# A second score pair brought forward on PE, with the routing steps, the seam to the network and the last experts' queues put in another order

## The chip, the cores and the metric

One core of a Trainium2 chip. The metric is the device time of one execution in microseconds (us), lower is better; runs are compared by their median. The engines are called PE (TensorE, matrix products), DVE (VectorE), ACT (ScalarE), POOL (GpSimd, which also issues the indirect DMAs) and SP (SyncE, which issues the other DMAs). From no change, a measurement of this kernel can tell about 0.2%.

## The reference, cut to what matters

A transformer block over 4 sequences of 512 rows of 512 columns: cross attention with 16 heads of 32 columns against a context of 256 columns, then a network of 64 routed experts (each row goes to 6 of them) and one shared expert.

```
x = x + xattn(layernorm(x), ctx_1024)          # q, k normed per head; 496 main keys and 16 dca keys,
                                               # each group with a softmax of its own, summed; then @ Wo
h = layernorm(x)
scores = softmax(h @ gate_w.T)                 # 64 experts
topk_w, topk_idx = top_k(scores, 6)            # weights normed to sum 1
buf[e, pos] = h[token]                         # at most C = 384 rows for each expert
eo = (silu(buf @ w_gate.T) * (buf @ w_up.T)) @ w_down.T     # F = 352
x = x + scattered sum of eo * topk_w + shared_swiglu(h)     # shared: FS = 704
```

All products are in fp32, made of three products of rounded parts (hi x hi, hi x lo, lo x hi), so that most matrices are cut into a `hi` part on ACT and a `lo` part on DVE.

## The kernel before, in words

The program has five instruction streams, one for each engine, written out in one order by hand and joined by semaphores. An engine runs its own stream strictly in order: whatever stands behind a waiting instruction waits too. Every function takes an index and returns at once when the index is out of range (`tile(j)`: 0 to 15, a block of 128 rows; `head(n)`: 0 to 63, one head of one sequence).

**The loop over heads.** After a front part, 16 units follow; unit u works on heads n = 4u to 4u+3, and beside them on one tile of each later or earlier stage: projections and turned keys for tiles u+4 to u+7, the turned attention output of tile u-4, its output product (`wo_product`), residual and second norm for tile u-5, and the routing of tile u-6. On PE a head is: `opened(n)` (the turned row maxima of head n, and the first pair of score products of head n+1), `half1(n)` (weigh 0 of the head before, the turned product of key block 0, weigh 1, turned product 1, and the second pair of scores of head n+1), `third_key(n)`, `fourth_key(n)`. Between them stand the products of the other tiles. The scores exist for their row maxima alone: the two banks of a pair are read by DVE (`maxima(n, half)`, lines 660 to 662), and PE may write the second pair only when the maxima of the first are taken. The maxima go back to PE to be turned (line 1403) and enter the turned products (line 1428) as four more rows; ACT takes the exp of each (line 1121).

**DVE in the loop.** Between the maxima stand `residual`, `rest` (the lo part of q or k, line 687, which waits for the hi part of ACT), `weighted` (the head's output by its sums, lines 671 to 673), `scales(u)` (the reciprocals of the norms, which POOL and ACT wait for), and the routing of one tile in pieces: `route_max`, `route_top`, `route_mask`, `take_pos`, `route_code` (lines 797 to 806), `route_slots` (812 to 818), `route_weights` (823, 825). PE makes the ranks of the routed rows in `route_pos`, from the mask and a running count that POOL keeps up (`counted_on`). POOL also joins the two outputs of each head (`join`), adds biases (`biased`, line 473), scales q and k (`scaled`, line 444) and writes the slot table by indirect DMA.

**The seam.** After unit 15, PE makes the last output products, first that of tile 11 (`WAIT1`) in two halves with the weighing of the last head between, then turns the attention output of tiles 12 to 15 (`a_last`, line 1470), with the first turned rows of the network (`transpose_chunk`) ahead of them. ACT and DVE cut these into hi and lo parts (`at_high`, `at_rest`, line 709) among the cuts of the network's first weights (`cut_x`, `cut_gu`).

**The network.** 72 items (8 of the shared expert, 64 routed ones with two blocks of 128 rows each) run in a fixed pipeline. For each routed item POOL gathers the rows, and adds the results onto the output by two indirect DMAs (`scatter`, line 2188), each pair only when the pair before has landed, since they add.

**Third blocks.** Experts with more than 256 rows (four with these inputs) get a third block each, in a loop at the end whose length is read from memory. SP loads its weights (`load`: gate and up weights, then down weights), POOL gathers and scatters (`gather`, line 2634; the scatter at line 2670 waits until the one before has landed), and the blocks 0 to 2 are started from within the last items (`gather_first`, `after`). The loads and gathers run three blocks ahead, so that some are for blocks that are not worked on.

## Time and profile before

| | |
|---|---|
| median of 3 runs | 1766.02 us (1765.25 to 1768.4) |
| the profiled execution | 1762.85 us |
| span of its instructions | 1761.1 us |
| mean granted TensorE clock | 0.982 |
| busy: PE / DVE / ACT / POOL | 96% / 62% / 58% / 43% of the span |

The span is the time from the first to the last instruction of the profiled execution. A busy PE isn't PE at its peak: a product also counts as busy at the lower clock. The share of busy time is a mean over very different parts: in the items PE has no idle time at all, in the front, at the seam and in the last 50 us it has.

### The profile page before, as it was taken

Reading aid. Unit: us, or ns where it says so; the run is one execution under the profiler, and the core shown is the slowest. Engines: PE = TensorE matmul, PEld = TensorE weight load, DVE = VectorE, ACT = ScalarE, POOL = GpSimd, SP = SyncE. Lnnn points to the kernel's source line nnn. Section 1 sums busy time; section 2 is a strip of 40 time slices with the busy share of each in tenths; the row PEclk is TensorE's granted clock in tenths of the full one; section 3 lists DMA queues with packets and bytes.
Section 4 is the critical chain, followed back from the end, with each engine's and each line's share of the span. In section 5 each row is a group of like instructions: output and inputs, shape, how many; then the busy total and the mean of one; then the engine's idle time right before and its main releaser. Section 6 shows DMA issues by size and latency. Waiting matters only on the chain. (4 is left out here: it accounts for less than half of the span.)

```text
span 1761.1 us, 35834 instructions
## 1 busy us (share of the span) xinstructions
PE 1693.0 (96%) x11782; PEld 1539.8 (87%) x11782; DVE 1090.3 (62%) x2157; ACT 1028.3 (58%) x1871; POOL 757.9 (43%) x719
## 2 busy tenths in 40 slices
PE   4899999999999999999999999999999999999995
PEld 3588888888888888989999999999999999999984
DVE  7555656777566665443666666666666666666664
ACT  4567766666545553222566666666666666666664
POOL 7513222334223230242245555555555555455554
PEclk8899999999899999999999999999999999999997
DMA  5543433433222532312577777777777777777766
GB/s 189 160 117 91 119 105 97 121 95 98 83 84 79 177 107 87 122 38 86 181 227 232 209 214 226 218 210 223 223 216 205 228 221 213 222 232 206 215 198 212
DMA packets 149083, 289.87 MB, mean 165 GB/s; under 512 B 29199, under 2 KB 66319, under 8 KB 139649
## 3 DMA queue, kind: packets, MB, share of 16 engines
q1 hardware_dynamic: 116112, 238.21, 41.9%
q0 software_dynamic: 32880, 50.51, 13.7%
q8 instruction: 50, 0.82, 0.2%
q14 instruction: 41, 0.33, 0.1%
HBM read 243.73 MB, written 64.52 MB: 175 GB/s over the span
## 5 line engine op out<-in xcount | busy, mean ns | idle before, releaser
L2188 POOL DMA_INDIRECT out<-y,ids_s x128 | 209.9, 1640 | 280.3 <-ACT y L2323 254.8
L2448 PE MATMUL ps<-xt_hi,gu_hi 128*128 128x256 f32 (+1 forms) x1856 | 303.5, 285 | 0.6 <-issue 0.6
L2448 PE MATMUL ps<-xt_lo,gu_hi 128*128 128x256 f32 (+1 forms) x1856 | 289.8, 278 | 0.0
L2448 PE MATMUL ps<-xt_hi,gu_lo 128*128 128x256 f32 (+1 forms) x1856 | 289.2, 278 | 0.0
L2223 DVE TENSOR_TENSOR gu_lo<-raw_gu,gu_hi 128x1408 fp32r<-128x1408 f32 (+2 forms) x132 | 214.6, 1625 | 112.5 <-ACT gu_hi L2220 109.3
L1121 ACT ACTIVATE prob<-ps 128x512 f32<-128x512 f32 x256 | 152.2, 597 | 191.4 <-PE ps L1428 169.6
L2448 PEld LDWEIGHTS ps<-xt_hi,gu_hi 128*128 128x128 f32 (+1 forms) x1856 | 250.6, 181 | 9.0 <-issue 3.0
L2448 PEld LDWEIGHTS ps<-xt_lo,gu_hi 128*128 128x128 f32 (+1 forms) x1856 | 244.4, 181 | 0.0
L2448 PEld LDWEIGHTS ps<-xt_hi,gu_lo 128*128 128x128 f32 (+1 forms) x1856 | 244.2, 181 | 0.0
L2168 POOL DMA_INDIRECT xg<-h_rows,ids_g x128 | 191.6, 1497 | 115.2 <-POOL ids_g L2163 50.6
L2280 ACT ACTIVATE h_hi<-h 128x256 fp32r<-128x256 f32 (+1 forms) x240 | 100.6, 419 | 224.0 <-DVE h L2349 223.4
L1447 PE MATMUL ps<-v_main,prob 128*128 128x33 f32 x1536 | 208.9, 274 | 0.0
L1447 PEld LDWEIGHTS ps<-v_main,prob 128*128 128x128 f32 x1536 | 194.8, 194 | 0.0
L660 DVE TENSOR_REDUCE nmax<-ps 128x2 fp32r<-128x992 f32 x128 | 152.2, 1189 | 58.2 <-PE ps L1418 54.4
L2271 ACT ACTIVATE sg<-ps 128x256 f32<-128x256 f32 (+1 forms) x240 | 91.0, 379 | 156.4 <-PE ps L2448 96.4
L2220 ACT ACTIVATE gu_hi<-raw_gu 128x1408 fp32r<-128x1408 f32 (+2 forms) x132 | 180.9, 1370 | 0.0
L464 POOL DMA_INDIRECT slot_table<-rows,slot x96 | 97.5, 1016 | 135.5 <-DVEq L1078 107.0
L2466 PE MATMUL ps<-d_hi,h_lo 128*128 128x512 f32 (+2 forms) x480 | 140.5, 398 | 0.0
L2349 DVE TENSOR_TENSOR h<-sg,ps 128x256 f32<-128x256 f32 (+1 forms) x240 | 99.3, 414 | 62.9 <-ACT sg L2271 55.4
L2466 PE MATMUL ps<-d_lo,h_hi 128*128 128x512 f32 (+1 forms) x480 | 137.3, 394 | 0.0
L2466 PE MATMUL ps<-d_hi,h_hi 128*128 128x512 f32 (+1 forms) x464 | 134.9, 397 | 0.0
L2354 DVE TENSOR_TENSOR h_lo<-h,h_hi 128x256 fp32r<-128x256 f32 (+1 forms) x240 | 101.2, 422 | 49.4 <-ACT h_hi L2280 48.0
(316 smaller groups left out, 3000.3 us busy)
## 6 DMA issues: line engine op xcount, KB each, us to landing
raw_gu<-in_w_gu SPq DMA_DIRECT2D x71, 1408.0 KB, 6.7
raw_d<-in_w_d SPq DMA_DIRECT2D x71, 512.0 KB
raw_d<-in_w_d SPq DMA_DIRECT2D x71, 192.0 KB
qs<-qk_rows SPq DMA_DIRECT2D x192, 64.0 KB, 2.2
ks<-qk_rows SPq DMA_DIRECT2D x192, 64.0 KB, 2.0
xa<-in_x SPq DMA_DIRECT2D x16, 256.0 KB, 3.0
qk_rows<-k_hi SPq DMA_DIRECT2D x16, 256.0 KB, 2.2
qk_rows<-k_lo SPq DMA_DIRECT2D x16, 256.0 KB, 2.5
```

Of the source, the lines that this page charges most:

```text
L660: dve.tensor_reduce(nmax[:, n % 2, t, 0], ps[:, SCB:SCB + 2, 0:MAIN], AX, ALU.max, negate=True)
L1121: act.activation(prob[:, n % 2, c, :], ps[:, STB + c % 2, :], ACT.Exp).then_inc(prob_ready.sem, 1)
L1447: last = pe.matmul(ps[:, POB, o:o + HD + 1], prow[:, c, :], v_main[:, b % 2, c, h, :], start=False, stop=c == T - 2)
L2168: pool.indirect_dma_start(out=B.xg[:, p, k, :], out_offset=None, in_=hbuf, in_offset=bass.IndirectOffsetOnAxis(B.ids_g[:, p, k:k + 1], 0), ...
L2188: pool.indirect_dma_start(out=out, out_offset=bass.IndirectOffsetOnAxis(B.ids_s[:, p, k:k + 1], 0), in_=B.y[:, p, k, :], in_offset=None, b ...
L2220: eng.activation(hi, raw, ACT.Copy).then_inc(gu_hi.sem, 1)
L2223: eng.tensor_tensor(lo, raw, hi.bitcast(F32), ALU.subtract).then_inc(gu_lo.sem, 1)
L2280: act.activation(B.h_hi[0:m, it.half, c, 0:W], B.h[0:m, (it.half * NF + c) % 2, 0:W], ACT.Copy).then_inc(h_hi.sem, 1)
L2349: dve.tensor_tensor(B.h[0:m, b, 0:W], B.sg[0:m, b, 0:W], gu_banks(it, c)[1], ALU.mult).then_inc(h_ready.sem, 1)
L2354: dve.tensor_tensor(B.h_lo[0:m, it.half, c, 0:W], B.h[0:m, (it.half * NF + c) % 2, 0:W], B.h_hi[0:m, it.half, c, 0:W].bitcast(F32), ALU.su ...
L2448: last = pe.matmul(gu_banks(it, c)[half], gu_columns(w, it, half, d, c), x[:, x_p, d, 0:W], start=i == 0, stop=i == len(steps) - 1)
L2466: last = pe.matmul(ps[:, Y0 + k % 2, :], h[0:m, p, c, k * P:(k + 1) * P], w[0:m, p, c, :], start=begins and i == 0, stop=ends and i == len ...
```

## The change

It changes no computation, only orders, in six places:

- **PE, loop.** `half1(n, early)` puts the second pair of scores of head n+1 behind the first turned product of head n instead of behind the second. It is early in head n where there is an output product (units 5 to 15), and in heads n+2 and n+3 where there is a q and k product (units 0 to 9). `route_pos` moves behind `third_key`, and `k_turned` behind it too in units 10 and on.
- **DVE, loop.** `weighted(n)` comes before `route_top`; `route_mask` behind `scales`; `route_code` behind the next maxima and `rest`; `route_slots` and `route_weights` behind `weighted(n + 2)`. POOL scales k and q before `counted_on`.
- **Seam.** The last head's four weighings come first; `a_last(WAIT1 + 1)` stands between the halves of the first output product, and both `a_last` stand before the network's first turned rows; ACT and DVE do `at_high` and `at_rest` of these before the cuts.
- **Items, POOL.** The copy of the scatter's indices is made before the wait for the last landing. The third block 2 is gathered one place earlier, and block 3 where block 2 was.
- **Third blocks.** Gathers run four ahead; down weights are loaded two ahead, behind the gate and up weights of three ahead; the weight and index columns are copied one block earlier.
- **ACT, last item.** `act_d(FIRST)` comes before `results`.

```diff
                 join(n)
                 scatter(u - 7, 2, 4)
-                counted_on(u - 6)
                 scaled(u + 5, kb, H, k_sum, kn_ready)
                 scaled(u + 5, qb, 0, q_sum, qn_ready)
+                counted_on(u - 6)
                 biased(u + 6, P, qb, bq, q_raw, q_bias)
                 join(n + 1)
                 scatter(u - 7, 4, 6)
...
                 ctx_rest(u + 6)
                 at_rest(u - 4)
                 maxima(n + 2, 1)
+                weighted(n)
                 route_top(u - 6)
-                weighted(n)
-                route_mask(u - 6)
                 maxima(n + 3, 0)
                 scales(u)
+                route_mask(u - 6)
                 maxima(n + 3, 1)
                 take_pos(u - 6)
                 weighted(n + 1)
-                route_code(u - 6)
                 maxima(n + 4, 0)
                 rest(u + 5, k_full, k_hi, k_lo, k_high, k_low, k_out)
+                route_code(u - 6)
+                maxima(n + 4, 1)
+                weighted(n + 2)
                 route_slots(u - 6)
-                maxima(n + 4, 1)
                 route_weights(u - 6)
-                weighted(n + 2)
                 summed(u + 6, sq_q, 0, q_sq, q_sum)
             item = net.item
             weighted(HEADS - 1)
+            at_rest(WAIT1 + 1)
             residual(WAIT1)
+            at_rest(WAIT1 + 2)
             net.cut_x(dve, item, 0, False)
             net.cut_x(dve, item, 1, False)
-            at_rest(WAIT1 + 1)
-            at_rest(WAIT1 + 2)
             net.cut_gu(dve, item, 0, False)
             residual(WAIT1 + 1)
             at_rest(WAIT1 + 3)
...
             item = net.item
+            at_high(WAIT1 + 1)
+            at_high(WAIT1 + 2)
             net.cut_x(act, item, 0, True)
             net.cut_x(act, item, 1, True)
-            at_high(WAIT1 + 1)
-            at_high(WAIT1 + 2)
             net.cut_gu(act, item, 0, True)
             at_high(WAIT1 + 3)
             net.cut_gu(act, item, 1, True)
...
                 shift_turned(n)
                 scores(n + 1, 0)
-            def half1(n):
+            def half1(n, early=False):
                 weigh(n - 1, 0)
                 turn_scores(n, 0)
+                if early:
+                    scores(n + 1, 1)
                 weigh(n - 1, 1)
                 turn_scores(n, 1)
-                scores(n + 1, 1)
+                if not early:
+                    scores(n + 1, 1)
             def third_key(n):
                 weigh(n - 1, 2)
...
                 if u == 5:
                     pe.wait_ge(pool_split, POOL_SPLIT["wo"])
                 wo_product(u - 5)
-                half1(n)
+                half1(n, tile(u - 5))
                 x_turned(u + 6)
                 route_logits(u - 6)
                 third_key(n)
...
                 opened(n + 2)
                 q_product(u + 6)
-                half1(n + 2)
+                half1(n + 2, tile(u + 6))
+                if tile(u + 6):
+                    k_turned(u + 5)
+                third_key(n + 2)
                 route_pos(u - 6)
-                k_turned(u + 5)
-                third_key(n + 2)
+                if not tile(u + 6):
+                    k_turned(u + 5)
                 fourth_key(n + 2)
                 opened(n + 3)
                 k_product(u + 6)
-                half1(n + 3)
+                half1(n + 3, tile(u + 6))
                 third_key(n + 3)
                 q_turned(u + 5)
                 h_turned(u - 5)
                 fourth_key(n + 3)
-
-            item = net.item
-            pe.wait_ge(at_lo.sem, at_lo.value(WAIT1, 1))
-            pe.wait_ge(h2T_in.sem, h2T_in.value(WAIT1 - 1, 1))
-            wo_half(WAIT1, 0)
-            weigh(HEADS - 1, 0)
-            weigh(HEADS - 1, 1)
-            wo_half(WAIT1, 1)
-            weigh(HEADS - 1, 2)
-            weigh(HEADS - 1, 3)
             def a_last(j, free, use):
                 pe.wait_ge(head_done.sem, head_done.value(HEADS - 1, 1))
...
                 wo_half(j, 0)
                 wo_half(j, 1)
+            item = net.item
+            for t in range(T):
+                weigh(HEADS - 1, t)
+            pe.wait_ge(at_lo.sem, at_lo.value(WAIT1, 1))
+            pe.wait_ge(h2T_in.sem, h2T_in.value(WAIT1 - 1, 1))
+            wo_half(WAIT1, 0)
+            a_last(WAIT1 + 1, v_ready, TILES - 1)
+            wo_half(WAIT1, 1)
+            pe.wait_ge(nmT_in.sem, nmT_in.value(HEADS - 1, 1))
+            a_last(WAIT1 + 2, pos_taken, GROUP1 - 1)
             pe.wait_ge(nmax_ready.sem, nmax_ready.value(HEADS - 1, 2))
             net.transpose_chunk(pe, item, 0)
             net.transpose_chunk(pe, item, 1)
-            a_last(WAIT1 + 1, v_ready, TILES - 1)
-            pe.wait_ge(nmT_in.sem, nmT_in.value(HEADS - 1, 1))
-            a_last(WAIT1 + 2, pos_taken, GROUP1 - 1)
             wo_last(WAIT1 + 1, pv_taken, HEADS - 1)
             a_last(WAIT1 + 3, at_lo, WAIT1 + 1)
             wo_last(WAIT1 + 2, x1_ready, WAIT1)
...
         if not it.exists or it.shared:
             return
         p = it.half
+        pool.tensor_copy(B.ids_s[:, p, 0:nb], slots_of(it, B.ids)).then_inc(s_copied.sem, 1)
         if it.known and it.e == SH_ITEMS:
             for k in range(nb):
                 pool.wait_ge(y_out[k].sem, y_out[k].value(TOKEN_BLOCKS // 2 - 1, 16))
         else:
             pool.wait_ge(added.sem, added.value(it.expert - 1, 16 * nb))
-        pool.tensor_copy(B.ids_s[:, p, 0:nb], slots_of(it, B.ids)).then_inc(s_copied.sem, 1)
         pool.wait_ge(y_taken.sem, y_taken.value(it.rows, nb))
         pool.wait_ge(s_copied.sem, s_copied.value(it.expert, 1))
         pool.sem_inc(passed, 1)
...
             gather(pool, it + 2)
             if not (it + 2).exists:
                 thirds["gather_first"](pool, (it + 2).e - ITEMS)
+            if not (it + 1).exists:
+                thirds["gather_first"](pool, 2)
             scatter(pool, it - 1)
         def after(it):
-            thirds["gather_first"](pool, 2)
+            thirds["gather_first"](pool, 3)
+            thirds["weight_column"](pool, FIRST)
+            thirds["row_column"](pool, FIRST)
             scatter(pool, it)
             thirds["y_freed"](pool)
...
             thirds["silu"](act, FIRST)
             thirds["act_gu"](act, FIRST + 1, 1)
             thirds["act_x"](act, FIRST + 1)
+            thirds["act_d"](act, FIRST)
             results(it)
-            thirds["act_d"](act, FIRST)
         drive(act, slot, after, side)
...
         return eng.value_load(over[0:1, bass.ds(b.j, 1)], min_val=0, max_val=E - 1)
     def sync(sp):
-        def load(e, b, gu_done, d_done):
-            src = ins["w_d"][bass.ds(e, 1)].rearrange("a f n -> (a f) n")
-            sp.wait_ge(*gu_done)
+        def load_gu(b, done, turn):
+            e = expert(sp, b)
+            sp.wait_ge(done.sem, done.value(turn, 2))
             sp.dma_start(B.raw_gu[:, b.p].rearrange("p a n -> p (a n)"),
                          ins["w_gu"][bass.ds(e, 1)].rearrange("a p n -> p (a n)")).then_inc(gu_in[b.p].sem, 16)
-            sp.wait_ge(*d_done)
+
+        def load_d(b, done, turn):
+            e = expert(sp, b)
+            src = ins["w_d"][bass.ds(e, 1)].rearrange("a f n -> (a f) n")
+            sp.wait_ge(done.sem, done.value(turn, 1))
             sp.dma_start(B.raw_d[:, b.p, 0:2, :], src[0:2 * P, :].rearrange("(c p) n -> p c n", p=P)).then_inc(d_in[b.p].sem, 16)
             sp.dma_start(B.raw_d[0:FCH[2][1], b.p, 2, :], src[2 * P:F, :]).then_inc(d_in[b.p].sem, 16)
         sp.wait_ge(A["over_made"], 1)
         for k in range(2):
-            load(expert(sp, FIRST + k), FIRST + k, (S.gu_lo.sem, S.gu_lo.value(LAST_ITEM.weights - 1 + k, 2)),
-                 (S.d_lo.sem, S.d_lo.value(LAST_ITEM.weights - 1 + k, 1)))
-        load(expert(sp, FIRST + 2), FIRST + 2, (gu_lo.sem, gu_lo.value(0, 2)), (d_lo.sem, d_lo.value(0, 1)))
+            load_gu(FIRST + k, S.gu_lo, LAST_ITEM.weights - 1 + k)
+            load_d(FIRST + k, S.d_lo, LAST_ITEM.weights - 1 + k)
+        load_gu(FIRST + 2, gu_lo, 0)
         def body(b):
-            e = expert(sp, b + 3)
-            load(e, b + 3, (gu_lo.sem, gu_lo.value(b.j + 1, 2)), (d_lo.sem, d_lo.value(b.j + 1, 1)))
+            load_gu(b + 3, gu_lo, b.j + 1)
+            load_d(b + 2, d_lo, b.j)
         each(sp, body)
     def gather(pool, b):
...
             in_offset=bass.IndirectOffsetOnAxis(B.ids3[:, b.p:b.p + 1], 0),
             bounds_check=N - 1, oob_is_err=False).then_inc(rows_in[b.p].sem, 16)
+    def weight_column(pool, b):
+        e = expert(pool, b)
+        pool.tensor_copy(B.wsl3[:, b.p:b.p + 1], B.w[:, bass.ds(e * CB + 2, 1)]).then_inc(w_copied.sem, 1)
+
+    def row_column(pool, b):
+        e = expert(pool, b)
+        pool.tensor_copy(B.ids3s[:, b.p:b.p + 1], B.ids[:, bass.ds(e * CB + 2, 1)]).then_inc(s_copied.sem, 1)
+
     def gather_first(pool, k):
         if k == 0:
...
         if k < 2:
             pool.wait_ge(S.xt_ready.sem, S.xt_ready.value(LAST_ITEM.rows - 1 + k, DC))
         else:
-            pool.wait_ge(xt_ready.sem, xt_ready.value(0, 1))
+            pool.wait_ge(xt_ready.sem, xt_ready.value(k - 2, 1))
         gather(pool, FIRST + k)
     def y_freed(pool):
...
     def gpsimd(pool):
         def body(b):
-            e = expert(pool, b)
-            pool.tensor_copy(B.wsl3[:, b.p:b.p + 1], B.w[:, bass.ds(e * CB + 2, 1)]).then_inc(w_copied.sem, 1)
-            pool.tensor_copy(B.ids3s[:, b.p:b.p + 1], B.ids[:, bass.ds(e * CB + 2, 1)]).then_inc(s_copied.sem, 1)
-            pool.wait_ge(xt_ready.sem, xt_ready.value(b.j + 1, 1))
-            gather(pool, b + 3)
+            pool.wait_ge(xt_ready.sem, xt_ready.value(b.j + 2, 1))
+            gather(pool, b + 4)
+            weight_column(pool, b + 1)
             if b.q:
                 pool.wait_ge(added.sem, added.value(b.j - 1, 16))
                 pool.sem_inc(y_free.sem, 1)
...
                 out=out, out_offset=bass.IndirectOffsetOnAxis(B.ids3s[:, b.p:b.p + 1], 0),
                 in_=B.y[:, b.p, 0, :], in_offset=None, bounds_check=N - 1, oob_is_err=False,
                 compute_op=ALU.add).then_inc(added.sem, 16)
+            row_column(pool, b + 1)
         many = each(pool, body)
         for p in range(2):
-            pool.wait_ge(rows_in[p].sem, (many + (4 - p)) // 2 * 16)
+            pool.wait_ge(rows_in[p].sem, (many + (5 - p)) // 2 * 16)
         pool.wait_ge(S.added.sem, S.added.value(LAST_ITEM.expert, 16 * nb))
         pool.sem_inc(passed, 1)
         with pool.If(many > 0):
...
             act.activation(B.y[:, b.p, 0, :], ps[:, Y0 + b.p, :], ACT.Copy, scale=B.wsl3[:, b.p:b.p + 1]).then_inc(y_taken.sem, 1)
         many = each(act, body)
         for p in range(2):
-            loads = (many + (4 - p)) // 2
-            act.wait_ge(gu_in[p].sem, loads * 16)
-            act.wait_ge(d_in[p].sem, loads * 32)
+            act.wait_ge(gu_in[p].sem, (many + (4 - p)) // 2 * 16)
+            act.wait_ge(d_in[p].sem, (many + (3 - p)) // 2 * 32)
         act.sem_inc(act_passed, 1)
     def dve_gu(dve, b, half):
```

## Rows read from the trace of the kernel before

**Rows 1.** List of waits of PE, 304 to 460 us: waited for, total, times, longest us.
```profile
PE ps L1403 <- DVEq L662: 2.6, 4, 0.8
```

**Rows 2.** Timeline, end of unit 8 and start of 9: start us, us, engine, line, operation, idle.
```profile
375.37 0.18 DVE L797 TENSOR_SCALAR tmp<-rank_of 128x64 f32<-128x64 f32 x1
...
377.05 0.22 DVE L806 TENSOR_TENSOR code<-code,tmp 128x64 f32<-128x64 f32 x1 [0.24 <-issue]
...
379.78 0.69 DVE L687 TENSOR_TENSOR k_lo<-k_full,k_hi 128x512 fp32r<-128x512 f32 x1 [1.07 <-ACT k_hi L1227]
...
380.80 1.65 POOL L473 TENSOR_TENSOR kb<-kb,bqk 128x512 f32<-128x512 f32 x1 [2.20 <-ACT kb L1129]
...
381.39 1.08 DVE L818 SCALAR_TENSOR_TENSOR slot<-code,slot_f 128x8 int32<-128x8 f32 x1
...
382.39 1.18 DVE L660 TENSOR_REDUCE nmax<-ps 128x2 fp32r<-128x992 f32 x1
...
383.75 0.61 PE L1403 MATMUL ps<-ident,nmax 128*32 128x128 f32 x4 [0.59 <-DVEq L662]
...
386.38 1.18 DVE L660 TENSOR_REDUCE nmax<-ps 128x2 fp32r<-128x992 f32 x1
...
388.23 0.48 PE L1428 MATMUL ps<-qs,ks 128*128 128x512 f32 x1
```

**Rows 3.** Timeline, unit 13.
```profile
538.49 0.41 PE L1444 MATMUL ps<-v_last,prob 128*128 128x66 f32 x2 [0.22 <-DVE pv L673]
...
541.65 1.09 ACT L1121 ACTIVATE prob<-ps 128x512 f32<-128x512 f32 x2
...
548.07 0.73 PE L1418 MATMUL ps<-ks,qs 96*128 96x512 f32 x2 [0.33 <-issue]
```

**Rows 4.** Windows: us, each engine's busy us (instructions), PE clock, DMA share, GB/s.
```profile
400.00:440.00 40.00, 39.40 (x276) 35.23 (x275) 28.60 (x78) 25.56 (x44) 15.94 (x19) 1.00 0.33 94
440.00:480.00 40.00, 38.83 (x228) 34.19 (x228) 23.29 (x63) 21.29 (x38) 12.46 (x16) 0.83 0.32 90
1000.00:1200.00 200.00, 200.00 (x1467) 188.41 (x1466) 128.60 (x225) 130.11 (x240) 109.27 (x89) 1.00 0.76 218
```

**Rows 5.** Timeline of PE, unit 10.
```profile
442.37 0.66 PE L1470 MATMUL ps<-ident,kb 128*128 128x128 f32 x4 [0.85 <-POOL kb L444]
```

**Rows 6.** Timeline, the seam.
```profile
611.50 0.60 ACT L1121 ACTIVATE prob<-ps 128x512 f32<-128x512 f32 x1 [0.96 <-PE ps L1428]
...
612.73 1.63 PE L1464 MATMUL ps<-wo,aT 128*128 128x512 f32 x6 [1.27 <-ACT h2T L1252]
...
620.57 1.09 PE L1470 MATMUL ps<-ident,ao_odd 128*128 128x128 f32 x8 [0.86 <-POOL ao_odd L453]
...
623.14 3.02 PE L1464 MATMUL ps<-wo,aT 128*128 128x512 f32 x12 [1.49 <-DVE aT L709]
...
632.17 0.69 DVE L709 TENSOR_TENSOR aT<-ps,aT 128x512 fp32r<-128x512 f32 x1
```

**Rows 7.** Timeline, the last 51 us.
```profile
1710.07 1.08 POOL L2183 COPY ids_s<-ids 128x2 int32<-128x2 int32 x1 [2.92 <-DMA out<-y,ids_s]
...
1712.01 4.75 POOL L2188 DMA_INDIRECT out<-y,ids_s  x1 [0.86 <-issue]
1712.16 3.15 DVE L2728 TENSOR_TENSOR gu_lo<-raw_gu,gu_hi 128x1408 fp32r<-128x1408 f32 x2
...
1717.07 1.83 POOL L2188 DMA_INDIRECT out<-y,ids_s  x1 [0.30 <-issue]
...
1726.18 1.96 POOL L2670 DMA_INDIRECT out<-y,ids3s  x1 [4.85 <-issue]
...
1728.11 1.12 PE L2769 MATMUL ps<-ident,xg 128*128 128x128 f32 x4 [7.59 <-DMA xg<-h_rows,ids]
...
1734.65 1.57 POOL L2670 DMA_INDIRECT out<-y,ids3s  x1 [4.09 <-ACT y L2718]
...
1751.48 1.57 POOL L2670 DMA_INDIRECT out<-y,ids3s  x1 [1.07 <-issue]
```

2 lines of the change are left out of this document (1 added, 1 removed).

## The prediction

> **What bounds the kernel now.** I read the page first. PE is busy in 96% of the span (the table above), so the kernel is a queue of matmuls and a change can only pay where PE waits, where its clock is low, or at the two ends. The table of windows over the whole span then shows where that is: the items from 760 to 1700 us have no idle at all (200 us busy of 200 [rows 4]), so nothing in them is priced; the loop over heads (85 to 612 us) has small waits, the seam behind it three, and the last 50 us are poor in PE work. The list of waits of PE in the loop names one regular wait: four times, 2.6 us in all, for the second row maxima of DVE [rows 1]. The timeline around it shows the order that causes it [rows 2], and that of later units shows two smaller ones [rows 3]. The windows show one stretch in which PE ran slowly without waiting: between 440 and 480 us the granted clock is 0.83 and only 228 matmuls fit, against 276 in the 40 us before [rows 4]; it begins behind a wait of 0.85 us [rows 5]. The timeline of the seam gives its three waits [rows 6]. For the end I read the chain that ended last and then the timeline of POOL's queue: the end is a chain of scatters, not of matmuls [rows 7].
>
> **The loop, boundaries of units 6 to 9 (heads n+3 to n+4).** The change moves the second score pair up by one weighing and one turned product (about 1.1 us), `route_code` from before `maxima(n+4,0)` to behind `rest`, and `route_slots` out to behind `weighted(n+2)`. What is late here is not the scores: DVE sits idle until ACT delivers `k_hi` (line 687 at 379.78 us), then runs `route_slots` and only then the second maxima at 382.39, for which PE waits until 383.75 [rows 2]. The order on ACT ahead of `k_hi` isn't touched, so `rest` starts at the same time, and the early scores alone gain nothing at this boundary. In place of `route_slots`, `route_code` now stands between: 375.37 to 377.27 is 1.9 us as it stands, some 1.7 without a disturbance, so 380.4 becomes 382.1. It would be done 0.3 us before the old start, if nothing stopped it. But line 818 took 1.08 us and ended with POOL's bias of `kb` (380.80 plus 1.65) [rows 2]: a DVE operation that reads two tensors of SBUF stood until POOL was through. After the change the bias comes at about 381.3 (its copy on ACT follows the exp of the second turned product, and that is 0.47 us later, since the scores stand before it), still within `route_code`, whose last four operations read two tensors each. I let it hold DVE for 1.0 us: the maxima start at 383.1 instead of 382.39, and PE waits 0.7 longer. Bounds: 0.3 gained (no collision), 1.3 lost (blocked twice). Four boundaries at 0.7: +2.8.
>
> The debt is carried on. From the end of line 660 at 383.6 to its next end at 387.6 DVE needed 4.0 us; with `route_slots` (1.2 us: 380.4 to 382.5 less 0.9 of blocking) it needs 5.2. PE reaches the early second scores at the end of the turned product at 388.23, so at 388.55, which is 4.8 us after 383.75 [rows 2]. So in the next head they wait some 0.4 us, where before they stood 1.1 us later and found the maxima done. Three boundaries, those whose unit still has a `summed` for q: +1.2 (bounds 0 and +2.4). Behind PE there, everything waits. At the boundary from unit 10 to 11 there is a `rest` for k but no bias: `route_code` is 0.5 longer than `route_slots`: +0.5. Part sum **+4.5**, bounds -1.2 and +8.
>
> **The loop, units 10 to 15.** Here the second scores keep their place (the test is on `tile(u + 6)`), but DVE's new order counts. In unit 13 PE waits 0.33 us at 548.07 for maxima that ran behind `route_code`; without it they end about 1.2 us sooner and the wait goes. The model of the profile gives 0.33, the starts of neighbouring products 0.5 more than usual; I take 0.45, four times: -1.8. At 538.49 PE waits 0.22 for `weighted(n)`, which now stands ahead of `route_top`. That gain is mostly lost again: `route_pos` no longer stands between the second and third turned product, and the third needs the exp at 541.65, late because of the table loads of `deviations` [rows 3]. I take -0.15 for each of five units. Part sum **-2.55**, bounds -4 and 0. Units 0 to 4 have no routing and no such waits: 0. At the heads with `q_product` or `k_product` in front, these cover the first maxima, so that the early scores find them done; without that cover each would cost up to the 1.2 us of line 660. In head n of units 5 and on, `wo_product` is the cover, apart from the 0.4 above.
>
> **Unit 10 and the clock.** PE waits 0.85 us for the scaled `kb` [rows 5]; 2 us later the clock is at its lower level, 1.2 GHz, and stays there: a mean of 0.83 over 40 us is 13.6 us at half, and 48 matmuls fewer than before at 0.145 us each are 7 us, of which 0.85 is the wait itself [rows 4]. I take 6.1 us. After the change the product of `kb` comes one weighing and one turned product (1.6 us) later, so that it finds `kb` (there at 442.37), and `counted_on` steps out of the way of the scaling. That removes the wait; but the third turned product steps up and waits some 0.5 for its exp (in unit 13 it would stand at 541.7, and the exp at 541.65 takes 0.5), and `route_pos` may wait for a mask that DVE now makes behind `scales`. So the idle is split, not gone: 0 for the wait itself (bounds -0.85 and +0.9), and for the clock **-6.1** if it stays up and 0 if it does not. Two waits of half the length, with a full product between them, speak for staying up. So does the seam, where 1.27, 0.86 and 1.49 us of idle within 12 us did not bring the clock down [rows 6].
>
> **The seam.** The idle is 1.27 (for `h2T`), 0.86 (for POOL's last join) and 1.49 us (for `aT_lo` behind two cuts) [rows 6], 3.6 in all. The weighings of the last head now come first and wait only for its last exp (611.50 plus 0.60), some 0.7 us; half an output product then hides `weighted` and the join, and `at_rest` ahead of the residual hides the third. What is late next is `at_rest(WAIT1 + 4)`: at 632.17 plus 0.69 it was just in time, and everything before it has now moved up by 3 us while the cuts ahead of it on DVE have not become shorter: 0.4 to 0.6. The first gate product moves up by **2.6** (bounds 1.0 and 3.6), and the weight loop behind it, PE-bound, keeps that.
>
> **The end.** Four experts have a third block. Their scatters start 8.4 us apart, each once the one before has landed: the first at 1726.18, the second at 1734.65, the fourth at 1751.48; 9.6 us after it the span ends [rows 7]. PE's wait of 7.59 us for gathered rows (1728.11) looks like the prize: POOL could gather that block only behind the scatters of the last routed expert, and now gathers it one place earlier. But the second scatter, whose product stood behind that wait, came 8.5 us after the first, no later than the fourth behind the third: the wait was hidden under the landing. What counts is when the last routed expert's scatters land. Their copy of indices started at 1710.07 as the scatter before landed, took 1.08, and the issue came at 1712.01; with the copy ahead of the wait it comes at about 1710.95. It then lasted 4.75 us, against 1.57 at 1734.65, because DVE ran two subtractions from 1712.16 to 1715.31 [rows 7]. These move up too, by some 1.7 us, the length of `act_d`, which ACT now does while it would wait for the results (an estimate). I take 1710.95 + 4.3 + 0.3 + 1.6 = 1717.2 at the one end, 1715.3 (it slips in between the two) at the other, against 1718.90: 1.7 to 3.6, so **-2.5**. The further `gather` on POOL (2 to 3 us) lies under the 8.4 us. SP now issues the gate and up weights without waiting behind the down weights, so they compete with these scatters earlier and less at the very end (one load of down weights is gone, one gather more): bounds for the part 0 and -5.
>
> The Trainium skill (SBUF — State Buffer, Who interferes with whom) says that a `tensor_tensor` with two SBUF inputs takes only the read side of the port that DVE shares with GpSimd, and infers that the making of descriptors isn't stopped by it. By that sentence the issue at 1712.01 would not have been held; the row of 4.75 us speaks against it. Under it the part would be that of rival (5).
>
> **Sum.** +4.5 - 2.55 - 6.1 - 2.6 - 2.5 = -9.25, against the profiled execution (1762.85, span 1761.1) 1753.6. The median of the runs shown is 3.2 us above it; I put the difference on the median: **1756.8 us**.
>
> **The rivals.** (1) The clock falls all the same, at unit 10 or at one of the boundaries, where PE now stands 1.3 to 1.7 us: all else as forecast, 1762.9. For it: the fall behind 0.85 us. Chance 0.34. (2) The other side: the boundary wait of units 6 to 9 itself brings the clock down, unit after unit. Each fall costs 6.1 us; with two it is 1769, with three 1775, so it decides from the third on, or from the second with the boundaries at the top of their bound. Against it: 1.27 us at the seam did nothing. 0.13. (3) `route_code` isn't stopped by POOL and the scores don't wait: the boundaries give -1.2, 1751.1. Against it: line 818. 0.12. (4) PE's wait at the end was real: -7.6 in place of -2.5, 1751.7; the scatters' even spacing speaks against it. 0.03. (5) DVE doesn't hold the issue: two of 1.57 us from 1710.95 end at 1714.4, so -4.5 at the end, 1754.8; 0.04, as the 4.75 us speak against it. My forecast: 0.34 as well, but with its neighbours (3) to (5), which differ by 6 us at most, by far the larger side.
>
> **How the numbers follow.** The forecast's own range is 1753 to 1761. The range for 8 in 10 takes in (3) to (5) below and (1) with its scatter above, 1751.5 to 1766.5, and leaves out (2) and the tails. From no change a measurement can tell about 0.2%, 3.5 us: faster is below 1762.5, slower above 1769.5. Faster: forecast, (3), (4), (5) and four tenths of (1): 0.65. Slower: the greater part of (2), and a little for unseen costs: 0.13. Same: 0.22.
>
> **What would show it.** The wait for the second maxima at the unit starts should grow from 0.6 to 0.8 us to about 1.4, with DVE's line 801 to 806 stretched beside POOL's bias; if it is gone, part one is wrong. Scores in head n of units 7 to 9 should wait about 0.4 us. The 0.33 waits in heads n+3 of units 11 to 14 should be gone. The clock between 100 and 700 us should be 1.00 throughout; a single 0.5 stretch makes it rival (1). The first gate product should start some 2.6 us earlier than the sum of the loop's changes says, and the four last scatters should still be 8.4 us apart with no wait of PE for rows before them. The prediction is wrong if the clock falls again, or if loads that start earlier push the landings apart.

## The result and the profile after

The changed kernel is slower by some 1%: 1784.64 us (median of 4, 1781.12 to 1787.78) against 1765.63 us (median of 4), a ratio of 1.0114 with a 95% interval of 1.0087 to 1.0141. The forecast was 1756.8 us. The profiled execution of the changed kernel took 1782.14 us, its span is 1780.4 us and its mean granted clock 0.969, against 1762.85, 1761.1 and 0.982.

The local prices come first, since they held. The list of waits of PE in the changed kernel, 300 to 460 us and then 460 to 620 us, answers to [rows 1, 3]:

```profile
PE ps L1403 <- DVEq L662: 5.4, 4, 1.4
PE ps L1418 <- DVEq L662: 1.4, 4, 0.4
PE ps L1428 <- ACT prob L1121: 0.7, 1, 0.7
```

```profile
PE ps L1428 <- ACT prob L1121: 1.8, 4, 0.5
```

The boundary wait is 1.4 us where 1.4 was forecast. The early scores wait 0.4 where 0.4 was, though four times and not three. The third turned product waits 0.5 for its exp as expected, in unit 10 it waits 0.7. The waits of 0.33 in head n+3 are gone. The timeline at the end of unit 8 shows the cause as forecast: DVE's line 803 was held until POOL's bias was through.

```profile
382.59 1.14 DVE L803 SCALAR_TENSOR_TENSOR code<-rank_of,code 128x64 f32<-128x64 f32 x1
...
382.31 1.34 POOL L473 TENSOR_TENSOR kb<-kb,bqk 128x512 f32<-128x512 f32 x1 [2.63 <-ACT kb L1129]
```

What failed is in the windows, which answer to [rows 4] (columns as there; the clock is the third number from the end):

```profile
400.00:440.00 40.00, 38.25 (x260) 33.93 (x258) 29.11 (x65) 23.05 (x42) 15.10 (x17) 1.00 0.33 96
440.00:480.00 40.00, 39.34 (x214) 34.89 (x213) 23.35 (x59) 20.48 (x36) 11.37 (x14) 0.74 0.27 77
480.00:540.00 60.00, 58.33 (x419) 51.70 (x417) 41.53 (x114) 33.20 (x55) 17.77 (x24) 1.00 0.30 84
540.00:580.00 40.00, 39.38 (x232) 35.00 (x231) 23.42 (x62) 18.09 (x33) 10.26 (x13) 0.79 0.22 64
580.00:620.00 40.00, 39.55 (x231) 35.12 (x230) 23.79 (x64) 19.21 (x33) 11.23 (x15) 0.79 0.54 185
620.00:660.00 40.00, 37.51 (x188) 32.32 (x187) 22.00 (x55) 16.33 (x24) 12.86 (x15) 0.79 0.14 47
660.00:700.00 40.00, 39.62 (x314) 37.58 (x314) 20.34 (x44) 21.68 (x45) 5.22 (x5) 1.00 0.27 93
```

PE is as busy as ever, but makes 232 products between 540 and 580 us where 279 fit at the rate of 480 to 540 (419 in 60 us). The clock record of the trace puts PE at its lower level (1.2 GHz) from 446.9 to 467.3, 549.3 to 566.3, 586.8 to 603.9 and 627.8 to 644.8 us: 71.7 us in four stretches, where the kernel before has one of 13.7 in this part (443.8 to 457.4). Such a stretch is called a fall below. Ahead of each stands a wait of the third turned product for its exp. These are the rows of units 10, 12 (no fall), 13 and 15:

```profile
446.21 0.50 PE L1428 MATMUL ps<-qs,ks 128*128 128x512 f32 x1 [0.66 <-ACT prob L1121]
...
517.44 0.50 PE L1428 MATMUL ps<-qs,ks 128*128 128x512 f32 x1 [0.46 <-ACT prob L1121]
...
547.26 0.50 PE L1428 MATMUL ps<-qs,ks 128*128 128x512 f32 x1 [0.45 <-ACT prob L1121]
547.61 0.33 PE L1540 MATMUL ps<-mask,upper 128*128 128x64 f32 x2
...
621.87 0.50 PE L1428 MATMUL ps<-qs,ks 128*128 128x512 f32 x1 [0.44 <-ACT prob L1121]
```

In units 13 and 14 the fall begins 2 us behind the start of this product, in unit 15 only 6 us behind it. The same 0.45 stands at 487.26 and 517.44 (units 11 and 12) with no fall behind it, so one such wait doesn't bring the clock down each time. By the starts of the units, unit 12, wholly at 2.4 GHz, took 30.2 us against 31.1 before the change; unit 14, with a fall, took 37.0 against 30.5.

### The profile page after: what moved, and what is told of

The parts are those of the page before. It is cut to its first block, busy times and chain, and to the rows that moved or that the text cites. A ratio compares the mean times of both kernels' runs of the same rounds, so it can differ in the third digit from the quotient of the medians.

```text
span 1780.4 us, 35877 instructions
## 1 busy us (share of the span) xinstructions
PE 1712.1 (96%) x11782; PEld 1558.7 (88%) x11782; DVE 1097.3 (62%) x2157; ACT 1030.1 (58%) x1871; POOL 778.6 (44%) x723
## 4 chain that ended last, share of the span: by engine, by line
PE 84%; issue 4%; DVE 3%; ACT 3%; DMA 2%; POOL 2%; DVEq 1%; POOLq 1%; ACTq 0%; SPq 0%
PE ps L2455 35%; PE ps L2473 18%; PE ps L1447 8%; PE ps L1455 4%; PE ps L1428 4%; PE ps L2432 3%; PE ps L1418 3%; PE ps L1444 2%; PE ps L1470 2%; PE ps L1403 1%; DMA out<-y,ids3s 1%; DMA out<-y,ids_s 1%; PE ps L2450 1%; DVE nmax L660 1%; ACT prob L1121 1%
## 5 line engine op out<-in xcount | busy, mean ns | idle before, releaser
L2191 POOL DMA_INDIRECT out<-y,ids_s x128 | 206.0, 1609 | 300.6 <-ACT y L2330 254.1
L1447 PE MATMUL ps<-v_main,prob 128*128 128x33 f32 x1536 | 217.7, 281 | 0.0
L1447 PEld LDWEIGHTS ps<-v_main,prob 128*128 128x128 f32 x1536 | 203.8, 202 | 0.0
```

Of the source, the lines that this page charges most:

```text
L1447: last = pe.matmul(ps[:, POB, o:o + HD + 1], prow[:, c, :], v_main[:, b % 2, c, h, :], start=False, stop=c == T - 2)
L2191: pool.indirect_dma_start(out=out, out_offset=bass.IndirectOffsetOnAxis(B.ids_s[:, p, k:k + 1], 0), in_=B.y[:, p, k, :], in_offset=None, b ...
```

## The experiments

Eighteen kernels ran. Each ratio is against the kernel before, timed beside them; its median there lay between 1762.3 and 1766.0 us, so that a difference of 4 us between kernels of the table that didn't run together says little. The last column names where the profiled execution ran at 1.2 GHz between the start of unit 10 and the first gate product.

| label | us, median | ratio (95%) | at 1.2 GHz |
|---|---|---|---|
| changed kernel | 1784.64 | 1.0087 to 1.0141 | units 10, 13, 14, end of 15 |
| e1_pe_order_late | 1809.28 | 1.0198 to 1.0327 | all six |
| e2_loop_as_before | 1760.19 | 0.9955 to 1.0020 | unit 10, seam |
| e3_loop_alone | 1790.23 | 1.0078 to 1.0209 | units 10, 13, 14, end of 15 |
| e4_seam_as_before | 1782.28 | 1.0083 to 1.0158 | units 13, 15 |
| e5_mask_back_too | 1808.25 | 1.0222 to 1.0261 | all six |
| e6_dve_pool_order_alone | 1803.38 | 1.0205 to 1.0259 | all six |
| e7_pe_order_alone | 1755.06 | 0.9933 to 0.9989 | seam |
| e8_waits_removed | 1800.87 | 1.0182 to 1.0226 | all six |
| e9_wait_filled | 1770.73 | 1.0003 to 1.0045 | unit 15 |
| e10_dve_head_n2_back | 1773.02 | 1.0017 to 1.0076 | units 10, 14, seam |
| e11_pe_order_and_late_boundary | 1764.06 | 0.9980 to 1.0014 | unit 14, seam |
| e12_weighted_first | 1803.83 | 1.0199 to 1.0247 | units 11 to 15 |
| e13_last_rows_first | 1756.19 | 0.9937 to 0.9981 | seam |
| e14_boundary_back_too | 1754.32 | 0.9908 to 0.9957 | seam |
| e15_pe_order_rows_first | 1756.07 | 0.9937 to 0.9982 | seam |
| e16_swap_filled | 1762.60 | 0.9983 to 1.0016 | seam |
| e17_seam_back_too | 1757.43 | 0.9939 to 0.9979 | seam, twice |
| e18_seam_filled | 1751.90 | 0.9900 to 0.9951 | none |

**Which part does it.** `e1`: in head n+2 of units 10 to 15, PE's order of before.

```diff
+                if not tile(u + 6):
+                    route_pos(u - 6)
+                k_turned(u + 5)
+                third_key(n + 2)
                 if tile(u + 6):
-                    k_turned(u + 5)
-                third_key(n + 2)
-                route_pos(u - 6)
-                if not tile(u + 6):
-                    k_turned(u + 5)
+                    route_pos(u - 6)
```

> Changed kernel with one order on PE put back, in units 10 to 15 alone: in head n+2 route_pos and k_turned stand between the second and the third turned product again, as before the change; everything else stays changed. Theory A (the four stretches at the lower clock in units 10, 13, 14 and at the seam come from the third turned product, which the change put in that place and which there waits 0.4 to 0.5 us for its exp in a stretch of small products): that wait is covered again, the granted clock between 460 and 660 us is 1.00 (at most one stretch), and the time falls by 3 or 4 times 6 to 8 us, to 1755 to 1764. Rival B (they come from DVE's order in the loop, or from the waits of 1.4 us at the boundaries of units 6 to 9): the four stretches stay and the time is 1780 to 1787. Rival C (they come from the new order of the seam): the stretches in the loop stay, 1780 or more.

> Changed kernel with the whole loop over heads as before the change, on PE, DVE and POOL; only the seam, the items' index copies, the third blocks and ACT's last item stay changed. Theory A and rival B alike: the clock in the loop is that of before, one stretch at the lower level behind unit 10, and the time is the kernel before less the two parts that lie behind the loop, 2.6 and 2.5 us in the prediction, 1759 to 1762 where the kernel before is 1765. Rival C (the seam's order brings the clock down): a stretch at the lower level at 600 to 650 us and a time of 1766 or more.

> Kernel before with the loop's part of the change alone (PE, DVE and POOL); the seam, the items, the third blocks and the end are as before. Theory A and rival B alike: the stretches at the lower clock in units 10, 13 and 14 are there, and the time is about 4 to 5 us above the changed kernel, 1786 to 1790. Rival C: no stretches of the clock beyond those of before, 1765 to 1772.

> Changed kernel with the seam as before the change (PE, DVE and ACT); the loop, the items, the third blocks and the end stay changed. Theory A and rival B alike: the stretches at the lower clock in units 10, 13 and 14 stay; the seam's own gain of 2.6 us is lost, 1785 to 1788, unless the last of the four stretches (627.8 to 644.8 us) hangs on the seam, then 1778 to 1781. Rival C: the stretches go and the time is below 1770.

`e2` and `e3` came out as A and B said (`e3` 0.2 us above its range): the loss is in the loop alone. `e2` has a fall of 6.8 us at the seam all the same. `e4` fits neither form. In its trace the third turned product waits 0.67 us in unit 10 and 0.46 in unit 14 with no fall behind either, and the last fall begins within a wait of 2.17 us for the rows of head 63 (up to 604.27 us), a cause of its own that comes back below. Theory A in its simple form fell with `e1`, which got worse by 25 us: with `route_pos` in its old place, PE waits there for a mask that DVE now makes behind `scales`. Its list of waits, 460 to 620 us:

```profile
PE ps L1540 <- DVE mask L789: 4.1, 4, 1.0
```

So the place of PE's product alone wasn't the cause; there was a longer wait behind the one that was removed.

**Which order on which engine.** `e5` is `e1` with the mask put back:

```diff
                 route_top(u - 6)
+                route_mask(u - 6)

                 maxima(n + 3, 0)
                 scales(u)
-                route_mask(u - 6)
```

> The kernel of e1_pe_order_late (route_pos and k_turned between the second and third turned product again in units 10 to 15) with one order on DVE put back as well: route_mask stands directly behind route_top, no longer behind scales. In e1_pe_order_late route_pos waited about 1.0 us for that mask in each of units 10 to 15, and the lower clock followed in each of the six. Theory A2 (in units 10 to 15 any wait of PE of some 0.5 us or more in the second half of head n+2 can bring the clock down; the change makes such a wait whichever of the two products comes first, since it moved both the product and the mask): now neither waits, no stretch at the lower clock in units 11 to 15, at most one in unit 10 (k_turned stands in its old place), and the time is 1752 to 1763. Rival B2 (the falls come from the early second scores or from the longer waits at the boundaries of units 6 to 9, which are still there): the stretches stay, 1780 to 1800.

> The kernel of e2_loop_as_before (seam, items and third blocks changed, loop as before) with DVE's and POOL's part of the loop's change alone; PE's order in the loop is that of before. Theory A2: route_pos stands between the second and third turned product and waits 1.0 us for the mask that DVE now makes behind scales, so the clock falls in each of units 10 to 15, as in e1_pe_order_late: six stretches and 1795 to 1808. Rival B2 in the form that the early second scores do it: no early scores here, so the clock in units 11 to 15 is 1.00 and the time is 1758 to 1768.

> The kernel of e2_loop_as_before with PE's part of the loop's change alone (early second scores, third turned product ahead of route_pos); DVE and POOL keep the order of before. Theory A2: the third turned product waits about 0.5 us for its exp in each of units 10 to 15 as in the changed kernel, and the clock falls in two to four of them: 1770 to 1782. Rival B2 in the form that DVE's order with its boundary waits does it: the waits of 1.4 us are gone here, the clock stays as in e2_loop_as_before, 1757 to 1763.

> The changed kernel with the orders put together so that none of the measured waits should stand: in units 10 to 15 route_pos before the third turned product, k_turned behind it, and route_mask directly behind route_top; in units 6 to 9 DVE's route_code ahead of the maxima and route_slots, route_weights in their old places (the boundary there as before the change). All else as changed. Theory A2: unit 10 has neither the wait for kb nor that for an exp, so there is no stretch at the lower clock between 300 and 600 us; the boundaries cost what they did before the change (-4.5 us against the changed kernel), and the time is 1747 to 1755. Rival B2: stretches stay in units 10 to 15, 1775 or more. If only the early second scores do harm, this kernel shows it too: 1765 or more.

`e6` came out as A2 said. `e7` did not: PE's part of the change alone, with the early scores and the third turned product ahead, gives no fall in units 10 to 15 and is 0.4% faster than the kernel before. `e5` and `e8` missed by 45 us, and their trace names what I had left in place. The list of waits of `e5`, 460 to 660 us:

```profile
PE ps L1418 <- DVEq L662: 5.0, 5, 1.0
```

Both kept `weighted(n)` ahead of `route_top`. `e12` is `e7` with this one exchange:

```diff
-                route_top(u - 6)
                 weighted(n)
+                route_top(u - 6)
                 route_mask(u - 6)
```

> The kernel of e7_pe_order_alone with one exchange on DVE: weighted(n) stands before route_top, as in the change; route_mask, scales and the boundary keep their old places. Theory A3: DVE then idles 0.5 us for the weighing of head n with 0.85 us of route_top still to do; the waits of 0.2 us for weighted(n) go, but the second scores of head n+3 or the third turned product wait 0.5 to 1.0 us in one piece in units 10 to 15, the clock falls in three to six of them, and the time is 1772 to 1805. Rival D3: this exchange is harmless, 1753 to 1758.

It cost 49 us. Five of its six waits of 1.0 us are followed by a fall, the one of unit 10 (446.15) isn't. The timeline of `e12` in unit 12 shows where they come from. First DVE, then PE:

```profile
514.57 0.21 DVE L671 RECIPROCAL rz<-ps 128x8 f32<-128x8 f32 x1 [0.52 <-PE ps L1447]
514.86 0.42 DVE L673 TENSOR_TENSOR pv<-ps,rz 128x256 f32<-128x256 f32 x1
515.20 0.15 DVE L768 RECIPROCAL zs<-zs 128x1 f32<-128x1 f32 x1
...
517.67 1.19 DVE L660 TENSOR_REDUCE nmax<-ps 128x2 fp32r<-128x992 f32 x1
...
519.05 0.74 PE L1418 MATMUL ps<-ks,qs 96*128 96x512 f32 x2 [1.00 <-DVEq L662]
```

In the old order `route_top` (some 0.85 us) fills DVE's 0.52 us until the weighing is done. In the new one DVE idles there and `route_top` and `route_mask` follow, so the next maxima end late and PE waits 1.0 us in one piece. In the changed kernel the mask was moved away as well, which lets the maxima start in time; `weighted(n)` comes early enough that PE's small waits in front vanish, and PE arrives at the third turned product 0.45 us before its exp. The small waits are these, in `e7`, unit 13:

```profile
532.52 0.41 PE L1444 MATMUL ps<-v_last,prob 128*128 128x66 f32 x2 [0.22 <-DVE pv L673]
...
535.08 0.73 PE L1418 MATMUL ps<-ks,qs 96*128 96x512 f32 x2
```

The first is 0.22 us. The second isn't marked as a wait, but that product starts 0.55 us behind the turned product before it, where 0.32 is usual. Two small waits had become one larger one.

**Is the idle stretch the cause?** `e9` and `e16` move nothing and add work:

```diff
                 weigh(n - 1, 1)
+                if more:
+                    for _ in range(2):
+                        again(n, 1)
                 turn_scores(n, 1)
```

`again` makes the same turned product into the same bank without signalling; `more` holds in head n+2 of units 10 to 15; `e16` has four repeats.

> The changed kernel with more work in one place and nothing moved: in head n+2 of units 10 to 15 PE makes the second turned product three times over (the same product into the same bank, signalled once), two products of 512 columns of 0.21 us each, or 2.6 us of work more over six units. They lie where PE otherwise waits some 0.45 us for the exp of the first turned product; DVE and ACT are both behind PE there, so nothing else should move. Theory A3 (this wait is what brings the clock down in units 13, 14, 15, since DVE's earlier weighted(n) took away the two small waits in front of it and left the idle in one piece): the wait shrinks to nothing, the clock in units 11 to 15 stays at 1.00, and the kernel with more work is faster than the changed one, 1758 to 1770; unit 10, with 0.88, may still fall. Rival C3 (the wait is a bystander; the clock follows something else in DVE's order): the stretches stay and the time is the changed kernel's plus 0 to 3 us, 1783 to 1788.

> The kernel of e12_weighted_first with more work and nothing moved: in head n+2 of units 10 to 15 PE makes the second turned product five times over instead of once, four more products of 512 columns of 0.21 us each, 5 us of work more in all, in the place where it waits 1.0 us for row maxima. Theory A3 (the idle stretch brings the clock down, whatever it waits for): the wait shrinks to 0.2 us, the clock in units 10 to 15 stays up in all or all but one, and the time is 1757 to 1770 against 1803.8. Rival C3 (something else in DVE's order brings it down): the five stretches stay and the time is 1800 or more.

Both came out as A3 said. Windows of `e12`, then of `e16`, which is the same kernel with some 5 us more work (24 products, which start 0.23 us apart):

```profile
460.00:500.00 40.00, 39.00 (x213) 34.62 (x212) 22.11 (x59) 17.82 (x30) 9.38 (x12) 0.74 0.25 74
500.00:540.00 40.00, 38.88 (x213) 34.20 (x212) 22.18 (x59) 16.65 (x28) 9.40 (x12) 0.75 0.22 65
540.00:580.00 40.00, 39.00 (x220) 34.38 (x218) 21.58 (x58) 16.66 (x28) 9.39 (x12) 0.78 0.21 60
```

```profile
460.00:500.00 40.00, 39.22 (x275) 34.53 (x275) 26.01 (x68) 19.96 (x34) 9.39 (x12) 1.00 0.27 77
500.00:540.00 40.00, 39.10 (x281) 34.29 (x279) 27.13 (x78) 22.73 (x40) 14.69 (x19) 1.00 0.29 84
540.00:580.00 40.00, 38.73 (x269) 33.54 (x269) 28.36 (x77) 22.82 (x38) 12.98 (x17) 1.00 0.26 72
```

More work, 41 us less time: PE's wait in head n+2 fell from 1.0 to some 0.15 us (by the starts of the products), and the five falls went. What is left are waits of 0.4 us in head n+3, which `e7` has in the same place, without a fall in either kernel. In `e9` the falls of units 10 to 14 went too, and 14 us with them, as this window shows (0.79 and 232 products in the changed kernel):

```profile
540.00:580.00 40.00, 39.51 (x285) 35.10 (x284) 28.83 (x83) 22.95 (x38) 12.29 (x17) 1.00 0.29 83
```

Rival C3, that DVE's order acts in another way than through what PE does in head n+2, is refuted by both. What the two can't separate is whether the shorter wait keeps the clock up or the longer products put into it; no run moved the one without the other. `e7` against `e12`, with the same products, speaks for the wait.

**What was left.** `e10` and `e11` take parts of DVE's order back:

> The changed kernel with DVE's order in head n+2 put back: route_top, weighted(n), route_mask, then the maxima and scales; PE's order and DVE's order at the boundary (route_code behind rest, route_slots behind weighted(n+2)) stay changed. Theory A3: head n+2 of units 10 to 15 is as in e7_pe_order_alone, with a wait of some 0.2 us for weighted(n) ahead of it and none of 0.5 for the exp, so the clock stays up there, and the time is that of e7_pe_order_alone plus the 4.5 of the boundaries less the 1.8 of head n+3, 1756 to 1762. Rival D3 (the boundary's order brings the clock down, units 6 to 9 or 10 to 15): stretches in several units, 1770 or more.

> The kernel of e7_pe_order_alone with DVE's new boundary order in units 10 to 15 alone (route_code behind rest, then the maxima, weighted(n+2), route_slots, route_weights); units 6 to 9 and head n+2 are as before the change. It takes away the waits of 0.33 us (0.5 to 0.67 us by the starts of neighbouring products) in head n+3 of units 11 to 14 and adds none. Theory A3 in its plain form: 1 to 2.5 us less than e7_pe_order_alone, 1752 to 1755, with the clock of e7_pe_order_alone. In the form of rival D3, or if any small wait that goes lets PE run into the next one and leaves the idle in one piece: the clock falls in some of units 11 to 15 and the time is 1760 or more.

Both missed their first reading by some 10 us; `e11` came out as its second. Both have a fall in unit 14 behind two small waits in head n+2 (0.22 us, and 0.2 by the starts) that `e7` has too, without a fall. So the waits of one place don't decide alone. The new boundary order in units 10 to 15 isn't free after all; why isn't settled, since `e14` and `e13` have it too and keep the clock, but with the products of `again` in front of it. `e9` had a fall of another origin, in head n+2 of unit 15:

```profile
599.71 1.22 PE L1418 MATMUL ps<-ks,qs 96*128 96x512 f32 x2 [2.74 <-DMA ks<-qk_rows]
```

SP issues the q and k rows of head 63 behind the network's first weights. `e13` moves `load_ring(63)` ahead of `net.load`, `e15` does so in `e7`, and `e14` is `e13` with DVE's old boundary order in units 6 to 9:

> The kernel of e9_wait_filled with one thing moved on SP: the loads of q and k rows of head 63 (six of 64 KB) are issued ahead of the network's first weights (6 MB) in unit 14, not behind them. In e9_wait_filled PE waited 2.7 us for them at 599.7 us in the profiled execution, and the clock was at its lower level for 34 us from there. Theory A3: the wait and the stretch go; -2.7 for the wait and about -10 for the clock, 1756 to 1762. Rival E4 (DMA traffic, not the order, makes the rows late, or the weights are late in turn): a wait for rows or for the network's first weights stays, 1766 or more.

> The kernel of e13_last_rows_first with DVE's order at the boundaries of units 6 to 9 as before the change (route_code ahead of the maxima, route_slots and route_weights in their old places); units 10 to 15 keep the new one. The waits of 1.4 us for the second maxima should go back to 0.7 and those of 0.4 us in head n disappear: 4.5 us less than e13_last_rows_first by the prediction's own sum, which the trace of the changed kernel bore out, so 1751 to 1758. If the two differ by less than 2 us, that part of the sum was wrong or is given back later.

> The kernel of e7_pe_order_alone with the rows of head 63 loaded ahead of the network's first weights. In the profiled execution of e7_pe_order_alone those rows came in time, but of its ten executions two took 1767 and 1774 us at a lower mean clock, the others 1751 to 1761. Theory A3 with the late rows as the reason of those two: median the same or 1 to 2 us less, 1752 to 1755, and no execution above 1765. If the late rows are not their reason: the same median and the same spread.

`e13` gained 14.5 us over `e9`: the wait and its fall are gone. `e15` did nothing for the median; none of its five executions lies above 1765 us, where two of ten did in `e7`, which is too few to tell. `e14` is 1.9 us below `e13`, with intervals that overlap, where the boundaries were priced at 4.5. The traces have it: units 6 to 9 take 151.0 us in `e13` (3.4 of them at 1.2 GHz) and 145.9 in `e14`, 5.1 less. But unit 6 of that execution of `e14` began 3.5 us later, by its clock in the front part, which varies from execution to execution, so that the medians show less than the loop gained.

**The seam.** `e17` is `e14` with the old seam, `e18` is `e14` with three products in front of the last head's weighings:

> The kernel of e14_boundary_back_too with the seam as before the change (PE, DVE and ACT). In e14_boundary_back_too the first gate product starts 31.4 us behind the first product of head 63, with 6.8 us at the lower clock between them; in the kernel before it is 30.4 us, at 2.4 GHz throughout. Theory F (the new seam gains some 2.5 us in waits and gives back 3.4 us, half of 6.8, by the clock): no stretch at the lower clock at the seam, 30.4 us from head to gate product, and a median within 0.15% of e14_boundary_back_too, 1751 to 1756. Prediction's own step (the new seam is worth 2.6 us): 30.4 us plus what the clock costs anyway, 1756 to 1759.

> The kernel of e14_boundary_back_too with three more products of 512 columns (the third turned product of head 63 again, into its own bank, 0.21 us each) ahead of the last head's weighings, where PE waits 0.69 us for the exp. Theory F: no stretch at the lower clock at the seam, 31.4 less some 3 us from head 63 to the first gate product, so 28 to 28.6 us, and a median of 1750 to 1753. Rival G (the 0.69 us is not its reason; the small weighings without other products between them are): the stretch of 6.8 us stays, 31.4 us, 1754 to 1756.

Windows over 596 to 640 us, of `e17`, `e14` and `e18` in turn:

```profile
596.00:640.00 44.00, 40.76 (x225) 34.94 (x225) 25.63 (x64) 18.70 (x31) 15.65 (x15) 0.84 0.14 49
```

```profile
596.00:640.00 44.00, 41.98 (x264) 37.26 (x263) 29.09 (x70) 21.41 (x36) 17.20 (x19) 0.92 0.19 67
```

```profile
596.00:640.00 44.00, 42.70 (x293) 37.88 (x293) 31.08 (x72) 23.61 (x40) 19.79 (x20) 1.00 0.23 80
```

Theory F was half right. The 0.69 us of wait ahead of the weighings does bring the clock down, as eight traces with this wait and a full clock ahead of it show (`e2`, `e7`, `e10`, `e11`, `e13` to `e16`: a fall of 6.8 us in each), and with it filled the way from head 63 to the first gate product is 28.3 us instead of 31.4. But the old seam falls as well, twice in this execution (35.7 us); that the kernel before had none there in its trace may have been chance, which one trace of each can't show. The new seam is worth some 3 us (1754.3 against 1757.4), with intervals that overlap. `e18` is the fastest kernel found, 0.74% below the kernel before (0.5 to 1.0%); its interval overlaps with that of `e14`, so that its gain over it rests on the trace.

## Why the prediction was wrong

**The step that failed** is the clock term of "Unit 10 and the clock": "-6.1 if it stays up", with "the idle is split, not gone" and "two waits of half the length, with a full product between them, speak for staying up". The fall of unit 10 stayed (20.5 us for 13.7) and three came to it, 58 us more at 1.2 GHz. What the runs showed in place of "the idle is split" is the contrary: in the second half of units 11 to 15 two small waits became one of 0.45 us, and where one of 1.0 us was made of it (`e12`), five of six units fell. Units 13 and 14 took 35.6 and 37.0 us for 30.5, and the way from the start of unit 10 to the first gate product is 20.8 us longer. Ahead of it 3.2 us were lost and behind it 4.7 won, which makes the +19.3 us. I had seen the third product's wait of 0.5 us in units 11 to 15 (it is in the part sum of -2.55), and priced it by its length alone. Its clock was asked for in unit 10 and at the boundaries of units 6 to 9 (rivals 1 and 2), never in units 11 to 15, where the kernel before had no fall. The 1.27 us at the seam [rows 6], of which rival (2) says that it "did nothing", and the 1.49 behind it misled me: `e17`, with waits of 1.3, 0.9 and 0.8 us there, fell twice.

**Units 6 to 9:** mechanism and size right: unit 6 starts 1.3 us earlier than before and unit 10 3.2 later, 4.5 in all. That the early scores alone gain nothing there holds too: units 6 to 9 take 146.0 us in `e7` and 145.5 in the kernel before.

**Units 10 to 15:** the waits of 0.33 and 0.22 went and unit 12 is shorter, at full clock, as forecast. The harm came with the 0.22: PE came early to the wait for the exp. Of the waits in unit 10, the third product's was taken as 0.5 and measured 0.66, and the fall of the kernel before begins 1.4 us behind 442.37, not 2.

**Seam:** 2.6 forecast, some 3 by `e17` against `e14`, both with falls. Without a fall it is 30.4 us from head 63 to the first gate product in the kernel before and 28.3 in `e18`, 2.1 less with three products more. In the changed kernel it can't be read, since half of it ran at the lower clock.

**End:** 2.5 forecast, within bounds of 0 and 5, and near the far one. From the first gate product to the end of the span it is 1125.3 us before and 1120.7 after, 4.7 less. From the first scatter of the last routed expert to the end it is 49.1 and 44.9. Timeline of POOL's queue, which answers to [rows 7]:

```profile
1735.54 2.42 POOL L2191 DMA_INDIRECT out<-y,ids_s  x1 [3.40 <-DMA out<-y,ids_s]
1738.27 1.56 POOL L2191 DMA_INDIRECT out<-y,ids_s  x1 [0.31 <-issue]
...
1747.42 1.75 POOL L2687 DMA_INDIRECT out<-y,ids3s  x1 [2.56 <-ACT y L2736]
...
1756.66 1.58 POOL L2687 DMA_INDIRECT out<-y,ids3s  x1 [2.17 <-ACT y L2736]
...
1763.85 1.86 POOL L2687 DMA_INDIRECT out<-y,ids3s  x1 [0.17 <-issue]
...
1769.73 1.58 POOL L2687 DMA_INDIRECT out<-y,ids3s  x1 [1.40 <-DMA out<-y,ids3s]
```

The first issue was held for less long (2.42 for 4.75 us). Of PE's wait for rows 2.1 us are left (7.59 before), where none was forecast. And the last scatters stand 9.2, 7.2 and 5.9 us apart, not 8.4 each: the spacing was no constant of landing. Why they come closer wasn't tested. `e2` fits both parts behind the loop together: among executions with the same mean clock (0.980, 0.982, 0.983, 0.987) it takes 3 to 6 us less than the kernel before, where 5.1 was forecast. Its median is only 2 us lower, with an interval that takes in no change, since its clock was lower in more of its executions.

**The rivals:** (2) came nearest in time, but through units 10 to 15, not through the boundaries of 6 to 9. Those waits of 1.4 us lie ahead of an output product and brought at most a fall of 3.4 us (`e13`, 310.5 to 313.9). (1) gave the mechanism a single fall. `e13` has the change's orders, and with the falls of units 10 to 15 out it takes 1756.2 us, near the forecast of 1756.8. That is in part luck: it has some 2.8 us of added products, the rows of head 63 come earlier, and its trace has falls of 3.4 and 6.8 us. But the sum as it stands, if the clock had stayed up, was about right.

## What to carry to other kernels

Where PE is 96% busy with small products, a wait's price is not its length: six waits of 1.0 us, one in each unit, cost `e12` 49 us against `e7`, eight times as much. Before an order is made tighter, ask of each wait it leaves whether several small ones become one, and where that one stands; a change that shortened the unit at full clock made the kernel slower. No rule that tells ahead which unit will fall came out of these runs. If such a wait can't be removed, a repeated product in it is cheap insurance (5 us of it gave back 41), and a kernel whose clock varies should be judged with the clock record beside the time, stretch by stretch.

## What the runs showed of the hardware

In the loop of the changed kernel, waits of 0.45 us in a stretch of short products were followed by a fall in three units of five, and one of 0.66 us in unit 10 by one; in `e4` 0.45 was followed by a fall once in four, and 0.67 by none. Waits of 1.0 us or more in head n+2 (`e1`, `e5`, `e6`, `e8`, `e12`) were followed by one in 29 of 30 units. A fall behind one of these waits took 17 to 27 us at 1.2 GHz, and a unit behind 10 with one was 5 to 9 us longer. Waits of 0.69 us ahead of the last head's weighings, the shortest products of the loop, were followed by a fall of 6.8 us in eight traces of eight where the clock had been up. Waits of 1.4 us at the unit's start mostly brought none.

POOL's scatter issue took 4.75 us where DVE's subtraction of two SBUF tensors ran from 0.15 us behind its start, 2.42 where one had begun 0.67 us ahead of it (1734.87), and 1.57 where none ran (1751.48, before). Where a subtraction was already running, the issue ended 1.4 to 1.5 us behind its end: 2.51 us at 1112.13 in the kernel before, with one that ended 1.0 us into it. Where it began 0.3 to 0.6 us behind the start of the issue, as in 64 issues of the items, the issue took only 1.57 to 1.65 us. One that began 0.03 us behind the start (1705.83 in `e7`) left it at 1.59, so that it stays open from when on a new one holds it. The Trainium skill (SBUF — State Buffer, Who interferes with whom) infers that such a subtraction doesn't stop the making of descriptors; the rows of 4.75, 2.51 and 2.42 us speak against it, though no run here tried it alone.
